# GpSimd's rstd of x2 ahead of the low halves in units 2 to 6, and VectorE's sums of read-back rows behind the last tile

## The reference, cut to what matters

```python
def xattn(q_in, kv, ...):            # 16 heads of 8, linear attention
    q = q_in @ Wq + bq; k = kv @ Wk + bk; v = kv @ Wv + bv
    qp = elu(q) + 1; kp = elu(k) + 1
    sums_t = sum over s <= t of outer(k_s, v_s)      # causal, in a scan
    out_t  = (sums_t . qp_t) / cumsum(qp)_t
    return out @ Wo + bo
x = x + xattn(layernorm(x), ctx, ...)
h = layernorm(x)                                     # "x2hat" in the kernel
bids = sigmoid(h @ conf_w.T + conf_b) * wealth       # 8 experts
two best experts per token, softmax of their two bids as weights
x = x + sum over the two of weight * ((silu(h @ gate.T) * (h @ up.T)) @ down.T)
```

## Time and profile before

| what | value |
|---|---|
| median of 3 runs | 331.06 us (330.39 to 331.72) |
| the profiled execution's own time | 329.64 us |
| its span in the trace | 327.9 us |
| PE busy | 296.4 us (90%) |
| DVE busy | 263.0 us (80%) |
| ACT busy | 234.5 us (72%) |
| POOL busy | 203.0 us (62%) |

### The profile page before, as it was taken

One profiled execution on the slowest core, in us unless ns is written; L12 is line 12 of the kernel. 1 busy time (PEld: TensorE's weight loads), 2 busy tenths in 40 slices (PEclk: granted clock), 3 DMA queues, 4 the chain that ended last, 5 costly groups with the idle time before them and its releaser, 6 DMA issues.

```text
span 327.9 us, 12647 instructions
## 1 busy us (share of the span) xinstructions
PE 296.4 (90%) x4611; PEld 245.1 (75%) x4611; DVE 263.0 (80%) x721; ACT 234.5 (72%) x468; POOL 203.0 (62%) x304
## 2 busy tenths in 40 slices
PE   7888998997999999799599999999999899999970
PEld 5467685775768686676289989988999899899930
DVE  6699999998999999788777697989567566666763
ACT  3698896988798897957259777667667577677620
POOL 5672333687878789788567657877554345444530
PEclk9999999999999999999899999999999999999996
DMA  7231413333243422401264334587959657533895
GB/s 215 81 105 57 128 37 88 108 100 110 81 116 101 128 78 53 130 30 42 49 105 72 64 67 93 161 175 195 171 156 207 185 160 155 83 67 109 269 309 190
DMA packets 49034, 39.59 MB, mean 121 GB/s; under 512 B 32710, under 2 KB 39756, under 8 KB 48976
## 3 DMA queue, kind: packets, MB, share of 16 engines
q1 hardware_dynamic: 43648, 28.62, 34.6%
q0 software_dynamic: 4320, 8.47, 9.7%
q10 hardware_dynamic: 1008, 1.70, 1.5%
HBM read 15.29 MB, written 12.21 MB: 84 GB/s over the span
## 4 chain that ended last, share of the span: by engine, by line
PE 38%; DVE 24%; POOL 10%; issue 9%; SPq 7%; DMA 6%; ACT 5%; POOLq 0%; DVEq 0%; ACTq 0%
DVE Pm L1108 5%; POOL by_expert L644 4%; PE bank L1676 4%; PE scores L1678 3%; PE scores L1676 3%; PE bank L1677 3%; PE scores L1677 3%; PE bank L1678 3%; PE bank L1697 3%; PE bank L1698 3%; PE bank L1705 3%; DVE Vexp L1081 2%; SPq L541 2%; DVE w_both L1175 2%; DVE Z L1089 2%
## 5 line engine op out<-in xcount | busy, mean ns | idle before, releaser
L644 POOL DMA_INDIRECT by_expert<-token_rows,rows_to x64 | 68.3, 1067 | 22.2 <-issue 17.9
L772 POOL DMA_INDIRECT by_token<-y_sb,row_meta x55 | 56.8, 1032 | 40.6 <-ACT y_sb L960 29.3
L1377 DVE SCALAR_TENSOR_TENSOR hid<-scores,silu 128x512 f32<-128x512 f32 x71 | 48.0, 689 | 30.8 <-PE scores L1678 27.4
L976 ACT ACTIVATE hid_hi<-hid 128x512 f16<-128x512 f32 x71 | 44.2, 628 | 20.1 <-DVE hid L1377 19.3
L969 ACT ACTIVATE silu<-bank 128x512 f32<-128x512 f32 x71 | 42.0, 596 | 22.1 <-PE bank L1678 20.0
L1383 DVE TENSOR_TENSOR Kexp<-hid,hid_hi 128x512 f16<-128x512 f32 x71 | 47.8, 688 | 8.0 <-ACT hid_hi L976 4.2
L1697 PE MATMUL bank<-w_both,hid_hi 128*128 x248 | 34.7, 219 | 2.2 <-issue 2.2
L1508 PEld LDWEIGHTS scores<-qT,Kexp 32*128 32x128 f32 x1024 | 31.4, 186 | 6.7 <-issue 6.7
L1508 PE MATMUL scores<-qT,Kexp 32*128 32x128 f32 (+1 forms) x1024 | 35.8, 276 | 0.0
L1698 PE MATMUL bank<-w_both,hid_hi 128*128 x248 | 34.5, 219 | 0.0
L1108 DVE TENSOR_SCALAR Pm<-scores 128x768 f32<-128x768 f32 x32 | 30.5, 954 | 2.5 <-PE scores L1508 2.1
(11 more groups left out here) (405 smaller groups left out, 789.7 us busy)
## 6 DMA issues: line engine op xcount, KB each, us to landing
w_raw<-in_w_pack_dram SPq DMA_DIRECT2D x24, 256.0 KB, 2.7
x_all<-in_x_tok_dram SPq DMA_DIRECT2D x8, 256.0 KB, 2.8
cT<-in_ctx_t_dram SPq DMA_DIRECT2D x8, 256.0 KB, 3.1
w_raw<-w_both SPq DMA_DIRECT2D x2, 768.0 KB, 3.9
Pm<-w_both SPq DMA_DIRECT2D x2, 768.0 KB, 5.1
Vexp<-w_both SPq DMA_DIRECT2D x2, 768.0 KB, 3.8
single_more<-w_both SPq DMA_DIRECT2D x2, 768.0 KB, 5.3
out_dram<-x_all ACTq DMA_DIRECT2D x6, 256.0 KB, 3.3
```

What stands on the lines that cost most here:

```text
L644: pool.indirect_dma_start(by_expert, bass.IndirectOffsetOnAxis(ap=rows_to[u % 2][:, s, b:b + 1], axis=0), token_rows[u % 2][:, b, s, :], N ...
L772: pool.indirect_dma_start(by_token, bass.IndirectOffsetOnAxis(ap=number, axis=0), y_sb[:, k, s, :], None, bounds_check=NT * TOP - 1, oob_i ...
L1377: dve.scalar_tensor_tensor(hid[:, slot, :], bank[2 + slot], 1.0 / WSCALE, silu[:, slot, :], ALU.mult, ALU.mult).then_inc(hid_done, 1)
```

## The change

Two edits. In GpSimd's body, units 2 to 6 now call `tail(u - 1)` first and `tail_rows(u - 2)` behind it; unit 7 keeps its order. In VectorE's end, the two last tiles are ordinary tiles again, and all sums of units 2 to 6 follow behind them.

```diff
             def body(u, par):
-                if u >= 2:
+                if last(u):
                     tail_rows(u - 2, par)
-                if last(u):
                     dispatch(u - 2, [0])
                 if not first(u):
                     tail(u - 1)
+                if u >= 2 and not last(u):
+                    tail_rows(u - 2, par)
                 if u == UNITS - 2:
                     dispatch(u - 2, range(UB))
                 elif u >= 2 and not last(u):
@@
-            for i in range(TILES - LAST_SINGLES):
-                tile_step(i, i % 4)
-            for i, u in zip(range(TILES - LAST_SINGLES, TILES), DVE_OUTS):
-                hidden(i, i % 4, 0)
-                add_first(u)
-                low(i, i % 4, 0)
-                add_second(u)
-            for u in DVE_OUTS[LAST_SINGLES:]:
+            tiles(dve, tile_step)
+            for u in DVE_OUTS:
                 add_first(u)
                 add_second(u)
```

## The result

The changed kernel takes 333.62 us, the median of 20 runs, against 331.25 us for the kernel before, the median of 20 runs beside it: a ratio of 1.0072, 95% interval 1.0044 to 1.0099, or 2.4 us slower (1.5 to 3.3). The forecast was 338.2 us. The side was right, and the size was three times too large: 7.1 us were forecast. The profiled execution took 333.17 us, 3.53 more than the one before. Now and then an execution is disturbed and takes longer; such ones count in the medians here but not in the ratios, and the profile of edit two alone, further down, fell into one, so its times are left out of the table.

The account below looks back on a forecast made before the run. VectorE paces the units and GpSimd's scatters set the end; the first scatter shifts 4L - 1.27 = +7.1 us with L = 2.1, edit two nothing, so 329.64 + 7.1 = 336.8, plus 1.42 gives 338.2 us median; range 333.5 to 342 (0.82).

Parts of the forecast that it names:

- VectorE keeps its turn: Rival: scans run through first, only the second half blocks w_both, 1.1 us per unit; 334.2 us, chance 0.12.
- What bounds the units, and what removes time: Units run at VectorE's pace; edit one removes 1.65 us in unit 1, 0.91 and 0.23 in unit 3.
- The base of 70.77 us for four units: Start of unit 2 to start of unit 6 without blocking: 71.91 - 0.91 - 0.23 us.
- halves and scans block each other: GpSimd's low halves and VectorE's scans, which read two SBUF tensors, take turns, lengthening every unit by L.
- side by side: Rival: halves and scans run without blocking, L = 0, first scatter 1.5 us earlier; 329.6 us, chance 0.12.
- absorbed: Rival: VectorE loses the time, but GpSimd's chain comes out as before within 1 us; 331 us, chance 0.06.
- The price L: VectorE's loss per unit from low halves on scans two to four: 2.1 us, between 1.65 and 2.44.
- From unit 6's aggregate to its first scatter: GpSimd's way in unit 6: 1.75 to the halves, 2.6 for the pair, 0.4 row numbers, 0.45 to scatter; 5.2 us.
- The way to the end: Unit 6's first scatter shifts by 4L - 1.27, +7.1 us, carried through SP's wait to the first tile and end.
- The bound of 1.3 us: Possible TensorE half-clock cost at the first tile, between nothing and 1.3 us; taken as nothing, kept for the range.
- VectorE's share in unit 7: Gets shorter because vdiff no longer lies on unit 6's low halves; earns nothing, as the first tile waits for rows.
- Edit two: VectorE's end: four moved sums, 2.7 us, hidden by the wait for unit 6's rows; nothing, 1 us either way.

Follow-up runs that it names:

- edit two alone: Only the reordered sums in VectorE's end, GpSimd's order as before, against the kernel before: 330.60 us, ratio 1.0012.
- the two kernels without the loss: Changed kernel with GpSimd memsets replacing five units' low halves, 325.91 us; kernel before with unit 2's halves held later and its second scatter unpaced, 327.37 us.
- memsets: Changed kernel with the low halves of units 0 to 4 replaced by GpSimd memsets that read nothing: 325.91 us, ratio 0.9849 against the kernel before.
- edit one alone: Only GpSimd's new order in the bodies, VectorE's end as before, against the kernel before: 333.43 us, ratio 1.0109.
- the last kernel of the table: Kernel before, unit 2's low halves waiting for unit 1's attention output and its second scatter no longer paced by ScalarE: 327.37 us, ratio 0.9896.

## Why the side was right and the size wrong

The stated range, 333.5 to 342, holds 333.62 by 0.12 us, and only because its low end had been stretched to a rival, "VectorE keeps its turn"; the forecast's own range, 335.4 to 341.9, does not hold it. That is luck.

- *What bounds the units, and what removes time.* Right. Unit 1's 1.65 us came back (0.22 and 0.16). ScalarE's wait for the shift is gone from units 2 to 6, and with it VectorE's 0.91 us. The base of 70.77 us for four units was met by the two kernels without the loss, 70.58 and 70.74.
- *That halves and scans block each other.* Right, and the rivals "side by side" and "absorbed" fall: four units grew to 75.13 us, and took 70.58 with memsets. The 0.23 us of unit 3 that the text counted for "side by side" was misread: in the kernel before, the first of those scans alone took 0.64 us (73.90 to 74.54), with the low halves running until 74.25, and the three others 1.02 together, so a half held up that scan too.
- *The price L.* This step failed. The text said that the halves come to lie on scans two to four "in every unit, since each time GpSimd is released by the same aggregate", and took 2.1 us a unit, 8.4 in all. Measured on the scans are 1.84 us in unit 2 and 0.92 in each of units 3 to 5, 4.60 in all; on the four units together 4.36 over the base of 70.77. The price of a full overlap was near, and within its bounds (1.84 against 1.65 to 2.44); what was wrong is that the overlap is full each time. From unit 3 on the shift came 0.05 us later against the scans and took 0.44 us instead of 0.20, so that the halves behind it asked 0.30 us later; their second half then lies beside the statistics. I had read one unit's release and taken it for all; the 0.33 us instruction of the earlier trace rows already showed such a lost turn. The run with the halves after two scans shows that the moment of asking decides. Why the shift came 0.05 us later is not settled: rstd took 1.04 us in unit 3 and 1.01 in unit 2, and no run tried that.
- *"VectorE keeps its turn".* Its 334.2 us is the nearest number, but its mechanism isn't what ran: scans were stretched in every unit, and w_both only in unit 6.
- *From unit 6's aggregate to its first scatter.* 6.05 us (128.68 to 134.73) instead of 5.2. The way to the halves took 2.03 us instead of 1.75, most of it a shift of 0.44 us; the row numbers of line 633 took 0.65 instead of 0.4 and end with the stretched w_both; from them to the scatter it took 0.85 instead of 0.45, for which no run gives the reason. The pair itself was 0.08 shorter than forecast.
- *The way to the end.* Right in kind: the first scatter is 4.22 us late, the first matmul 4.75. The clock was at 0.50 there as before and cost nothing more: from first matmul to second hid 3.56 us, against 4.25. The bound of 1.3 us was needed: edit one alone took 5.40, which is 1.15 more than before.
- *VectorE's share in unit 7.* Wrong, without effect on the sum: it was to get shorter, but the low halves that had lain on vdiff came to lie on chosen (2.81 us), and from line zser_oT's row at the start of unit 7 to its next row it took 23.51 us (141.87 to 165.38) instead of 21.81. The first tile still waited for its rows, 0.60 us.
- *Edit two.* Right: the four moved sums and the four behind them end at 321.51, and unit 6's sum still waits 0.72 us for its rows. The run of it alone gives 1.0012.

The error of 4.58 us, 338.2 against 333.62, adds up along the prediction's own path: unit 2 started 0.27 later than forecast; four units took 75.13 instead of 79.17, so -4.04; to unit 6's aggregate +0.01; to the scatter +0.85; from there to the end 198.44 us instead of the 199.13 of before, -0.69; and the median lies 0.45 us above the profiled execution where 1.42 was added, -0.97. The sum is -4.57. The step on L is the one large term; the others, 1.13 us up and 1.66 us down, nearly cancel.

What stays open is the last 0.7 us and the 0.97: the profiles differ by 3.5 us, the medians by 2.4. From the second hid to the last sum the eight profiles read here take between 155.8 and 158.8 us, with no change in that stretch but edit two's order, so single profiles can't settle a microsecond there.

## What to carry to other kernels

When a reading GpSimd instruction is moved under VectorE work with two SBUF inputs, price it unit by unit and write down at which of VectorE's instructions it asks: here the small instruction ahead of the halves came 0.05 us later and the halves 0.30, and the price was 0.92 in place of 1.84 us. The loss showed as longer busy time, not as a wait, so compare the length of the same line in both kernels. The cheap place for such an instruction here was beside VectorE work on PSUM or on one input; where GpSimd idled anyway, one wait that held it until then came with 1.1% less time (0.5 to 1.8%), of which the traces explain a part, while the reorder lost 0.7%.

## What was not expected of the hardware

- Turns are not handed out evenly in these traces. In the run with halves after four scans, w_both got in between the two halves (1.02 us); but chosen in unit 7 sat through both and took 2.81 us, and vdiff had done the same with 2.61. Both had started before the halves, chosen 0.47 us and vdiff 0.31, which is more than the 0.19 and 0.18 us that they take alone; what held them before the halves began is not shown.
- An idle TensorE does not by itself say what clock follows. After 3.37 us of idle the kernel before ran at 0.50, after 4.55 us edit one alone did; the last kernel of the table idled 3.38 us ahead of the router's matmuls at the same place, and its granted clock was 1.00 in every stretch of 2 us from 158 to 174. The first tile took 2.90 us to its second hid there, against 3.45 to 5.40 in the five profiles with the clock at 0.50.
